# A graph kernel's message stage: picks compared from slot codes that a DMA spreads over the partitions, in place of transposed picks

## The reference, cut to what matters

```
msg  = x[src]                                           # 100000 x 128
sums = segment_sum(msg, dst * 8 + etype)                # per node and type
h    = (sums / max(cnt, 1)).reshape(n, 8, 128)
x'   = einsum('nrf,rfo->no', h, W) + x @ root + bias    # relu between the layers
```

## Time and profile before

| what | value |
|---|---|
| median of 3 runs | 5284.67 us (5283.87 to 5290.28) |
| the profiled execution | 5296.44 us, its span 5294.7 us |
| busy share of the span: PE, PEld, DVE, ACT, POOL | 79%, 61%, 69%, 41%, 50% |
| mean granted TensorE clock | 0.872 of 2.4 GHz |
| the three A stretches | 422.9, 420.5 and 418.0 us |
| instructions | 118295 |

### The profile page before, as it was taken

How to read it: one execution, slowest core, us unless ns; L and a number is a source line. 1 busy time by engine, 2 the same in 40 slices (tenths; PEclk the granted TensorE clock), 3 DMA queues, 4 the chain that set the end, 5 groups by cost and what they waited for, 6 DMA issues and landing times.

```text
span 5294.7 us, 118295 instructions
## 1 busy us (share of the span) xinstructions
PE 4173.4 (79%) x30835; PEld 3240.1 (61%) x30836; DVE 3672.2 (69%) x8050; ACT 2158.7 (41%) x5004; POOL 2660.8 (50%) x2369
## 2 busy tenths in 40 slices
PE   3478888877888566666667888899988999988997
PEld 2445555555554455555454777776777777777776
DVE  8967777777777777777774566566566676566667
ACT  0014344444432111111113555576555576555575
POOL 3878788888700777777771000475000475000476
PEclk8557788888878778878886999999999999999999
DMA  1011111111100423223221455675455675455676
GB/s 40 28 44 37 40 40 40 40 41 39 32 0 0 104 74 77 74 73 77 74 74 10 145 171 170 180 208 162 135 171 172 184 208 168 131 172 172 183 208 182
DMA packets 672518, 553.38 MB, mean 105 GB/s; under 512 B 158723, under 2 KB 584885, under 8 KB 672462
## 3 DMA queue, kind: packets, MB, share of 16 engines
q0 software_dynamic: 111712, 277.47, 18.4%
q1 hardware_dynamic: 560750, 275.24, 17.9%
HBM read 307.55 MB, written 244.94 MB: 104 GB/s over the span
## 4 chain that ended last, share of the span: by engine, by line
PE 53%; issue 14%; POOL 14%; DVE 13%; DMA 4%; DVEq 1%; ACT 0%; POOLq 0%; SPq 0%; ACTq 0%
PE ps L799 24%; PE ps L796 23%; POOL y_sb L610 12%; DMA mid<-msgs,block_idx 4%; PE ps L1055 4%; DVE y_sb L1218 3%; DVE mid L1410 2%; DVE mid L1405 2%; POOL mid L622 2%; PE ps L894 1%; DVE mid L1379 1%; DVE mid L1371 1%; DVE y_sb L1245 0%; DVE mid L1583 0%; DMA y_sb<-in_x_dram,idx_st 0%
## 5 line engine op out<-in xcount | busy, mean ns | idle before, releaser
L796 PE MATMUL ps<-mid 128*128 128x128 f32 (+3 forms) x8452 | 1555.8, 320 | 333.0 <-DVE mid L1405 244.8
L634 ACT ACTIVATE mid<-ps 128x512 f32<-128x512 f16 (+4 forms) x2484 | 1084.8, 464 | 1400.2 <-PE ps L796 674.7
L622 POOL DMA_INDIRECT mid<-msgs,block_idx x750 | 715.4, 954 | 1748.7 <-DMA msgs<-mid 1501.3
L796 PEld LDWEIGHTS ps<-mid 128*128 128x128 f32 (+3 forms) x8452 | 919.8, 169 | 626.3 <-issue 298.7
L599 POOL DMA_INDIRECT slot_rows<-y_sb,row_st x784 | 1102.9, 1407 | 272.2 <-issue 230.2
L610 POOL DMA_INDIRECT y_sb<-in_x_dram,idx_st x808 | 824.9, 1021 | 528.2 <-ACT idx_st L634 279.3
L799 PE MATMUL ps<-y_sb,mid 128*128 x6552 | 945.8, 287 | 134.6 <-issue 132.7
L799 PEld LDWEIGHTS ps<-y_sb,mid 128*128 128x128 f32 x6552 | 793.9, 191 | 260.0 <-issue 213.7
L1583 DVE TENSOR_SCALAR mid<-iota,slot_lo,slot_w 128x128 f32<-128x128 f32 x2250 | 666.2, 379 | 311.8 <-PE ps L796 302.7
L799 PE MATMUL ps<-y_sb 128*128 128x193 f32 x1616 | 429.1, 421 | 280.3 <-DVE mid L1509 191.1
L634 ACT ACTIVATE y_sb<-ps 128x512 bf16<-128x512 f16 (+2 forms) x375 | 205.1, 554 | 1037.2 <-PE ps L976 888.2
(11 more groups left out here) (242 smaller groups left out, 3670.7 us busy)
## 6 DMA issues: line engine op xcount, KB each, us to landing
msgs<-mid SPq DMA_DIRECT2D x819, 256.0 KB, 2.3
y_sb<-slot_rows SPq DMA_DIRECT2D x101, 268.0 KB
y_sb<-in_edge_attr_dram SPq DMA_DIRECT2D x54, 256.0 KB
y_sb<-in_x_dram,idx_st POOLq DMA_INDIRECT x808
slot_rows<-y_sb,row_st POOLq DMA_INDIRECT x784
mid<-msgs,block_idx POOLq DMA_INDIRECT x750, 3.7
y_sb<-in_edge_attr_dram SPq DMA_DIRECT2D x44, 224.0 KB
mid<-in_L_gnn_W_dram SPq DMA_DIRECT2D x3, 512.0 KB
```

What stands on the lines that cost most here:

```text
L622: nc.gpsimd.indirect_dma_start(out=rows[:, s % RB, :], out_offset=None, in_=msg_blocks, in_offset=bass.IndirectOffsetOnAxis(ap=block_idx[: ...
L634: return nc.scalar.activation(o, i, func, **kw)
L796: return nc.tensor.matmul(o, a, b, start=False, stop=False, skip_group_check=True)
```

## The change

The compare is made with the source rows on the partitions from the start, so that nothing has to be turned in the loop:

- Once, before layer 0's nodes are finished, TensorE turns `a_code` with nine transposes, VectorE subtracts one and writes `code_st`, and SyncE stores it to a DRAM tensor `codes` (one row of 128 f16 codes for each tile) and waits until that has landed.
- For each group SyncE loads the group's 512 codes (1 KB) into every partition (`to_broadcast`, 128 KB), into one of four buffers `a_codes`, which reuse `a_code` and `iota_h`. `in_turns_led(sp, AG, load_codes, store_msgs, 4, 3)` issues the load of g + 3 and then the store of g.
- VectorE `pick_slots` waits for the load of its group, and compares the codes with the partition's number, straight to f32 `a_pick` (four buffers now).
- `turn_picks` and `copy_pick` are gone; `a_sel` and `iota1_h` too.

```diff
+        codes = nc.dram_tensor("codes", [-(-TA // P) * P, P], F16).ap()
+        code_groups = codes[0:TA, :].rearrange("(g k) p -> g (k p)", k=BLK)
...
-        a_sel = take(2 * BLK * P, F16).rearrange("p (b k m) -> p b k m", b=4, k=BLK)
-        a_pick = take(2 * BLK * P).rearrange("p (b m) -> p b m", b=2)
+        a_pick = take(4 * BLK * P).rearrange("p (b m) -> p b m", b=4)
+        code_st = take(4 * BLK * D)[:, 0:-(-TA // P) * P // 2].bitcast(F16)
...
+        a_codes = [t[:, q * BLK * P:(q + 1) * BLK * P] for t in (a_code, iota_h) for q in range(2)]
...
@@ SyncE
+            last = TA // P
+            sp.wait_ge(S["codes_made"], 2)
+            sp.dma_start(codes[0:last * P, :].rearrange("(q t) p -> t q p", t=P),
+                         code_st[:, 0:last * P].rearrange("t (q p) -> t q p", p=P)).then_inc(S["codes_stored"], 16)
+            sp.dma_start(codes[last * P:TA, :], code_st[0:TA - last * P, last * P:(last + 1) * P]
+                         ).then_inc(S["codes_stored"], 16)
+            sp.wait_ge(S["codes_stored"], 32)
             for l in range(3):
+                def load_codes(g, b, n):
+                    wait_used(sp, S["a_picked"], g + (l * AG - 3))
+                    sp.dma_start(a_codes[b], code_groups[ds(g, 1), :].to_broadcast([P, BLK * P])
+                                 ).then_inc(code_in[b], 16)
...
-                in_turns(sp, AG, store_msgs, 4)
+                in_turns_led(sp, AG, load_codes, store_msgs, 4, 3)
@@ ScalarE
-                def copy_pick(g, b, n):
-                    par = b % 2
-                    act.wait_ge(S["a_turned"], g + (l * AG + 1))
-                    wait_used(act, S["a_made"], g + (l * AG - 1))
-                    copy(a_pick[:, par, :], A_TRN[par]).then_inc(S["a_copied"], 1)
-                in_turns_ahead(act, AG, copy_pick, take_odd, 4)
+                in_turns(act, AG, take_odd, 4)
@@ TensorE
+            pe.wait_ge(S["a_coded"], 1)
+            for q in range(-(-TA // P)):
+                n = min(P, TA - q * P)
+                t = nc.tensor.transpose(CODES_T[0:n, q * P:(q + 1) * P], a_code[:, q * P:q * P + n], ident_h[:, :])
+            t.then_inc(S["codes_turned"], 1)
             pe.wait_ge(S["bias_made"], 1)
...
-                def turn_picks(g, b, n):
-                    par = b % 2
-                    pe.wait_ge(S["a_picked"], g + (l * AG + 1))
-                    wait_used(pe, S["a_copied"], g + (l * AG - 1))
-                    for k in range(BLK):
-                        t = nc.tensor.transpose(A_TRN[par][:, P * k:P * (k + 1)], a_sel[:, b, k, :], ident_h[:, :])
-                    t.then_inc(S["a_turned"], 1)
                 def make_msgs(g, b, n):
-                    pe.wait_ge(S["a_copied"], g + (l * AG + 1))
+                    pe.wait_ge(S["a_picked"], g + (l * AG + 1))
...
-                in_turns_ahead(pe, AG, turn_picks, make_msgs, 4)
+                in_turns(pe, AG, make_msgs, 4)
@@ VectorE
+            dve.wait_ge(S["codes_turned"], 1)
+            whole_tiles = TA // P * P
+            v.tensor_scalar(code_st[:, 0:whole_tiles], CODES_T[:, 0:whole_tiles], -1.0, None, ALU.add
+                            ).then_inc(S["codes_made"], 1)
+            rest = (slice(0, TA - whole_tiles), slice(whole_tiles, whole_tiles + P))
+            v.tensor_scalar(code_st[rest], CODES_T[rest], -1.0, None, ALU.add).then_inc(S["codes_made"], 1)
...
                 def pick_slots(g, b, n):
-                    wait_used(dve, S["a_turned"], g + (l * AG - 3))
-                    v.tensor_tensor(a_sel[:, b, :, :], iota1_h[:, :].unsqueeze(1).to_broadcast([P, BLK, P]),
-                                    a_code[:, ds(g * BLK, BLK)].unsqueeze(2).to_broadcast([P, BLK, P]), ALU.is_equal
+                    dve.wait_ge(code_in[b], 16 * n + (stored_before(l, b) + 16))
+                    wait_used(dve, S["a_made"], g + (l * AG - 3))
+                    v.tensor_scalar(a_pick[:, b, :], a_codes[b], part[:, 0:1], None, ALU.is_equal
                                     ).then_inc(S["a_picked"], 1)
```

More of the change, by code:

```diff
@@ L140, in gnn_resnorm @@
         not_same = sb("not_same", [P, 1])
-        iota1_h = sb("iota1_h", [P, P], F16)
         part = sb("part", [P, 1])
@@ L313, in gnn_resnorm @@
         late = at
-        a_sel = take(2 * BLK * P, F16).rearrange("p (b k m) -> p b k m", b=4, k=BLK)
-        a_pick = take(2 * BLK * P).rearrange("p (b m) -> p b m", b=2)
+        a_pick = take(4 * BLK * P).rearrange("p (b m) -> p b m", b=4)
+        code_st = take(4 * BLK * D)[:, 0:-(-TA // P) * P // 2].bitcast(F16)
+        at -= 4 * BLK * D
         a_out = take(4 * BLK * D).rearrange("p (b f) -> p b f", b=4)
+        a_codes = [t[:, q * BLK * P:(q + 1) * BLK * P] for t in (a_code, iota_h) for q in range(2)]
         at = late
@@ L332, in gnn_resnorm @@
         LOOK = ps[:, 4, 0:SPH * BLK * R * 3]
-        A_TRN = [ps[:, par, 0:256].bitcast(F16) for par in range(2)]
+        CODES_T = ps[:, 2:4, :].rearrange("p a b -> p (a b)").bitcast(F16)
         assert ACC == 7 and 2 * SUM <= 512 and CH == 8 and BLK == 4 and 4 * F1 <= 512
@@ L345, in gnn_resnorm @@
                  "sel_made pair_made tile_added s_picked s_turned s_copied s_used s_looked s_taken b_weighted w_step "
-                 "a_coded pos_step bias_made nodes_cleared chunk_begun n_staged n_turned n_copied n_made "
+                 "a_coded codes_turned codes_made codes_stored pos_step bias_made nodes_cleared chunk_begun n_staged n_turned n_copied n_made "
                  "n_taken n_stat bn_step stat_begun sd_made rstd_made h_made h_made_act h_turned h_copied "
-                 "y_made y_taken_act y_taken_dve a_picked a_turned a_copied a_made a_taken_dve a_taken_act "
+                 "y_made y_taken_act y_taken_dve a_picked a_made a_taken_dve a_taken_act "
                  "b_picked b_squared b_picked_act b_used neg_made out_made out_in")
@@ L355, in gnn_resnorm @@
         stored = [sem(f"stored{i}") for i in range(4)]
+        code_in = [sem(f"code_in{i}") for i in range(4)]
         b_gathered = [sem(f"b_gathered{i}") for i in range(RB)]
@@ L1023, in node_sums @@
                                  stop=True).then_inc(S["n_made"], 1)
-            pe.wait_ge(S["a_coded"], 1)
             staggered(pe, NW, ((turn_sums, 0), (node_sums, 0)))
@@ L1064, in make_msgs @@
                     for k in range(BLK):
-                        m = whole(ps[:, 2 + b, P * k:P * (k + 1)], a_pick[:, par, P * k:P * (k + 1)],
+                        m = whole(ps[:, 2 + b, P * k:P * (k + 1)], a_pick[:, b, P * k:P * (k + 1)],
                                   y_sb[:, ds(at[k] * D, D)])
                     m.then_inc(S["a_made"], 1)
-                in_turns_ahead(pe, AG, turn_picks, make_msgs, 4)
+                in_turns(pe, AG, make_msgs, 4)
                 pe.wait_ge(S["a_taken_act"], taken_before(l + 1, 1))
@@ L1275, in _ @@
                                  ALU.add, ALU.mult))
-            then(v.tensor_copy(iota1_h[:, :], iota1[:, :]))
             for k in range(BLK):
```

## The result

The changed kernel takes 6856.33 us (median, 6854.49 to 6870.72), the kernel before beside it 5287.48 us: a ratio of 1.297 (95% interval 1.294 to 1.300), 1569 us slower. The forecast was 6200 us, with a range from 5840 to 6740 us. The direction and the mechanism came out, the size did not: the time lies 116 us above the range.

The account below looks back on a forecast made before the run. TensorE was taken to bound stage A at 3.08 us per pair; a 5.3 us ring adds 409.5 x 2.2 = 901 us. 5296.4 + 901 + 9 + 3.5 = 6210 us profiled, stated as 6200 us, range 5840 to 6740 us.

Parts of the forecast that it names:

- What bounds the kernel now: Message stage A, 1261.3 us over three layers, is bound by TensorE alone: 1.54 us per group, 3.08 us per pair.
- The ring through SyncE's order: In A, loads queue behind stores that wait for VectorE's take, which waits for picks: 5.3 us per pair; chance 0.65.
- Landing of the load: In A's ring, a load of codes lands 1.9 to 2.5 us after its issue; 2.5 us taken.
- store's fixed part: Fixed 1.5 us of a store's 2.3 us; by it a load of codes would land 1.9 us after issue.
- rival 3: Loads in A: 128 reads of one same KB are slow, adding 3.2 us per ring; pair 8.5 us, 7500 us; chance 0.09.
- SyncE's issues: In A's ring, SyncE sees the take and issues store, load, store: 0.1 + 3 x 0.45 = 1.45 us.
- Transfers served in their order: A pair's four transfers share the DMA engines; the last lands 4.1 us after the take, 4.6 with loads' fixed part.
- queue model: A pair's four transfers served in order on the DMA engines; at 4.6 us landing the ring is 5.9 us.
- Pick 0.49 us, take 0.694 us, hand-overs: VectorE's part of A's ring, with three hand-overs of about 0.05 us: 1.33 us.
- The low clock: TensorE's clock falls in A; 4.9 us per pair at half clock, under the ring, adds nothing; B +3 us, three times.
- Once: Before layer 0's node work: nine transposes, two VectorE passes and two hand-overs in the path, about +3.5 us.
- rival 5: In A the ring doesn't bind; TensorE sets 1.31 us per group without transposes: -188 us, 5097 us; chance 0.03.

Follow-up runs that it names:

- e1: Changed kernel with VectorE picking one group ahead of its take instead of three; 5598.8 us, ratio 1.058 to the kernel before.
- e2: Changed kernel with the loads of codes issued by ScalarE instead of SyncE, still three groups ahead; 5439.85 us, ratio 1.029 to the kernel before.
- e3: Changed kernel with SyncE's loads issued six groups ahead instead of three; 5229.82 us, ratio 0.990 to the kernel before.
- e4: Changed kernel with each partition loading a row of its own instead of one shared row (wrong codes); 6392.92 us, ratio 1.209 to the kernel before.
- e6: Changed kernel with two of the four matmuls of each group in A left out; 6848.67 us, ratio 1.296 to the kernel before.
- e9: Changed kernel with all loads of codes but the first four left out (wrong messages); 5211.67 us, ratio 0.984 to the kernel before.
- e7: Changed kernel with the edits of e3 and e4 together: loads six groups ahead, different rows; 5251.26 us, ratio 0.993 to the kernel before.
- e10: e9 with constant bucket numbers, so without TensorE's register load and register addresses; 4807.07 us, ratio 0.907 to the kernel before.
- e11: e3 with one load of codes per two groups, plus one register load of eight bucket numbers per two groups; 5169.92 us, ratio 0.976 to the kernel before.

## Why the prediction was wrong in size and right in mechanism

- **What bounds the kernel now.** Right: A was TensorE, and only A changed.
- **The ring through SyncE's order.** Right, and shown by e1, e2 and e3, each of which opens it at another place: 1257, 1417 and 1627 us less than the changed kernel.
- **Landing of the load, taken as 2.5 us.** This is the term of the sum that was mis-sized most. It is 3.53 us in the chain: +1.03 us x 409.5 = +420 us. Of the 3.5 us some 2.0 are a load of different rows alone, 1.0 the one row that all partitions read (both from the first loads, e4), and 0.5 what the burst around it adds. e4's 2.35 us are near my 2.5, but with some luck: alone such a load takes 2.0 us, close to the 1.9 of my store's fixed part, and the rest is waiting in the burst, which I had in another term. I had the slow row as rival 3, but at 3.2 us for a ring and as a case of its own with 0.09. It should have widened the range from its smaller sizes on, since no row of the trace bounded it.
- **SyncE's issues, taken as 0.1 + 3 x 0.45 = 1.45 us.** The load of g+5 starts 7.44 - 5.52 = 1.92 us after the first store's start in the burst shown (2.02 us on average over the 116 bursts from 4300 to 5100 us). Each issue takes 0.60 to 0.66 us from start to start, though the instruction is 0.34 to 0.40 us long. I had added the register work of the earlier trace rows and not the gaps between them and around the wait: +0.47 us, or +190 us. The trace of before had only SyncE's lonely stores, but the row of lengths was taken as a price of a turn.
- **Transfers served in their order.** I counted this as the other bound (4.1 to 4.6 us from the take to the last landing) and took 3.95 us, by issue and landing alone. The queue model held better than that. e4's trace, one burst and its picks:

```profile
4600.77 0.69 DVE L1588 COPY mid<-ps 128x512 f32<-128x512 f32 x1
4601.62 0.40 SPq L558 DMA_DIRECT2D msgs<-mid  x1
4602.29 0.34 SPq L551 DMA_DIRECT2D a_code<-codes  x1
4602.90 0.40 SPq L558 DMA_DIRECT2D msgs<-mid  x1
...
4603.56 0.34 SPq L551 DMA_DIRECT2D a_code<-codes  x1
4604.66 0.49 DVE L1581 TENSOR_SCALAR mid<-a_code,part 128x512 f32<-128x512 f16 x1 [3.20 <-DMA a_code<-codes]
...
4606.18 0.49 DVE L1581 TENSOR_SCALAR mid<-a_code,part 128x512 f32<-128x512 f16 x1 [1.03 <-DMA a_code<-codes]
```

  The last pick starts 4.72 us after the take (4601.46 to 4606.18 us). Issue and a lone landing would give 2.1 + 2.0 = 4.1 us, the model 4.6. The DMA engines in this burst, then in one of the changed kernel (its second store is issued at 4606.78, its last load at 4607.44 us); the last two columns are DMA share and GB/s:

```profile
4602.60:4605.40 2.80, 0.69 (x5) 0.43 (x3) 0.49 (x1) 0.60 (x1) 0.00 (x0) 0.91 0.92 262
```

```profile
4606.60:4607.40 0.80, 0.80 (x5) 0.71 (x4) 0.00 (x0) 0.00 (x0) 0.00 (x0) 0.50 0.95 283
4607.40:4608.60 1.20, 0.21 (x1) 0.00 (x0) 0.00 (x0) 0.60 (x1) 0.00 (x0) 0.50 0.48 132
```

  e4's four transfers fill the engines for 2.8 us, though the average over A is 0.47. So the last load waits for what lies ahead of it, by some half a microsecond. In the changed kernel the engines are full for the first store. Then, while the first load of one row and the second store are being served, they are half idle for 1.2 us. The slow row holds up the engines without giving them work.
- **Pick 0.49 us, take 0.694 us, hand-overs.** The pick, of a form that no row showed, is 489 ns. From the start of the pick to the next store's issue it is 1.26 us (4610.80 to 4612.06 us), against 1.33 forecast:

```profile
L1579 DVE TENSOR_SCALAR mid<-a_code,part x411: 480/489/492, 2922.7 to 6499.6; 128x512 f32<-128x512 f16 x137
```

- **The low clock.** It fell in A as forecast (0.57 to 0.64), and adds nothing by itself (e6). B starts lower; B, the y stage and the end are 8.7 us longer in all three layers together, against 9 forecast. TensorE's first work in B is at a lower clock now; the same 50 matmuls take 5.82 us in the trace of before:

```profile
3848.11 7.75 PE L1081 MATMUL ps<-mid 128*128 128x128 f32 x50 [0.88 <-DVE mid L1586]
```

- **Once.** 3.83 us from the start of the casts of `a_code` to TensorE's first node work, before it was 1.79: +2.0 us, against +3.5:

```profile
2812.25 1.41 DVE L1531 CAST a_code<-ps 128x364 f16<-128x364 f32 x3
2813.71 0.91 PEld L1023 LDWEIGHTS ps<-ident_h,a_code 128*128 128x128 f16 x9 [4.20 <-DVE a_code L1531]
...
2816.08 0.47 PE L1030 MATMUL ps<-ident,y_sb 128*128 128x128 f32 x1 [1.23 <-DVE w_ea L1540]
```

- **The other side, rival 5.** Its condition (a ring under 3.08 us per pair) was rightly held unlikely, but its price was wrong. I took TensorE without transposes as 1.15 + 0.16 = 1.31 us per group. e9 measures 1.43, e7 1.49 us. The 0.16 us of issue was a remainder: by e10, the register load of the bucket numbers (0.33 us on TensorE's queue) and the register addresses stand between the groups and had lain partly under the transposes. How they share the gap is open. The trace of before has the row, and I did not look at this queue:

```profile
L803 PEldq TENSOR_LOAD <-tile_bucket x819: 327/332/738, 2928.3 to 4942.6; - x164
```

In sum the pair is 5.3 + 1.03 (landing) + 0.47 (issues) + 0.1 (left) = 6.9 us. The last 0.1 us was not followed up. e4 removes the slow row and lands at 5.78 us. That is 5.3 + 0.47 by the issues, but it is also near the 5.9 us of my own queue model, and the time alone does not tell these two apart. The engines are full through e4's burst, so that quicker issues alone would have gained less than 0.47 us there; no run tried it. The step that failed is the landing of the load: a broadcast was priced like any load, at 2.5 us, and it took 3.53.

The Trainium skill, DMA: Bandwidth & Descriptors (Anatomy of one DMA), gives about 2.0 us plus the bytes over 436 GB/s for transfers that GpSimd issues; I used it for one of SyncE's, an estimate of 2.3 us for 128 KB. A load of different rows took 2.0 us alone and 2.35 us in the burst (e4), and the broadcast 3.0 and 3.5 us. The page's advice to issue early and wait late (Rules for kernel authors) is what e3 does, and e3's 5229.82 us against 6856.33 agree.

## What to carry to other kernels

A lead in a loop counts only from the place where the transfer is issued in its queue: look at what the issuing engine waits for ahead of it, and let the issuing queue run further ahead (here six groups) than the engine that uses the data (three). Draw the ring that goes through all in-order queues, and pay for one turn of it with each instruction's distance from start to start, not its length. Look at the DMA share inside a burst and not only at its average. When a cover such as a transpose is taken off a busy engine, look first for what lay under it on the same queue.

## What the runs showed of the hardware

- 128 partitions that read one and the same row of 1 KB from DRAM get it 3.5 us after the issue in a burst and 3.0 us after it alone; when each reads a row of its own it is 2.35 and 2.0 us (e4). While such a load is served in a burst, the DMA engines are half idle (0.48, against 0.92 in e4's burst). With six groups of lead the landings still differ (3.8 us on e3's loads, 2.9 on e7's, medians), but the time does not. Why the row is slow was not tried.
- Four f32 matmuls of 128 columns, with a register load of four numbers and register addresses for each group, follow each other every 1.43 us (e9), 0.46 us of that between the last weight load of a group and the first of the next; with constant addresses every 0.93 us (e10, where the stores had filled the DMA engines).
- TensorE at its lower clock, 106 of 300 us busy, did not hold up a ring that runs through DMA landings (e6), and the clock was 1.00 again in A once the ring was opened (e3).
- Stores of 256 KB in packets of 512 B filled the DMA engines to 0.96 at 282 GB/s (e10), stores and loads together to 0.98 at 289 GB/s (e11).
